# Two graph networks on one core: later key batches, sigmoids ahead of the sum copy, and another order of work at the networks' border

## What is computed

```python
h = relu(layernorm(x))
h = relu(h @ enc_w1.T + b) @ enc_w2.T + b            # encoder
for w in conv_w:                                     # 5 layers of one GRU cell
    agg = segment_sum((h @ w)[src], dst)
    r, z = sigmoid(...), sigmoid(...)                # from agg @ wih.T and h @ whh.T
    n = tanh(i_n + r * h_n)
    h = (1 - z) * n + z * h
x = x + sigmoid(relu(relu(h) @ dec_w1.T + b) @ dec_w2.T + b)   # decoder
g = relu(layernorm(x))                               # second network
g = relu(A @ g @ W1.T + b1)                          # A: adjacency with degree scales
x = x + A @ g @ W2.T + b2
```

## Time and profile before

| | us |
|---|---|
| runs (3) | 798.94, 802.02, 803.88 |
| median | 802.02 |
| the profiled execution's own time | 802.24 |
| its span in the trace | 799.7 |
| TensorE busy in the span | 735.3 |

### The profile page before, as it was taken

One profiled execution on the slowest core, in us unless ns is written; L12 is line 12 of the kernel. 1 busy time (PEld: TensorE's weight loads), 2 busy tenths in 40 slices (PEclk: granted clock), 3 DMA queues, 4 the chain that ended last, 5 costly groups with the idle time before them and its releaser, 6 DMA issues.

```text
span 799.7 us, 9315 instructions
## 1 busy us (share of the span) xinstructions
PE 735.3 (92%) x3802; PEld 375.1 (47%) x3802; DVE 329.2 (41%) x652; ACT 322.9 (40%) x446; POOL 39.2 (5%) x49
## 2 busy tenths in 40 slices
PE   2379999899989999999999999999997799999996
PEld 2256656434534445444444444444444445555443
DVE  4999998452402325032250322545645521213101
ACT  0378988662433425243262422523345411221000
POOL 4300000000000000000000000120011210000000
PEclk9989999999999999999999999999999999999999
DMA  6000010342310224003140031420002000000001
GB/s 170 7 1 2 1 70 2 55 100 46 70 23 1 60 54 75 11 7 73 35 83 2 14 66 35 85 80 1 1 0 97 1 1 1 1 1 2 26 14 44
DMA packets 78553, 28.37 MB, mean 35 GB/s; under 512 B 70100, under 2 KB 77653, under 8 KB 78378
## 3 DMA queue, kind: packets, MB, share of 16 engines
q1 hardware_dynamic: 75738, 26.01, 15.1%
q10 hardware_dynamic: 2528, 1.06, 0.6%
q0 software_dynamic: 240, 0.66, 0.3%
HBM read 8.03 MB, written 2.60 MB: 13 GB/s over the span
## 4 chain that ended last, share of the span: by engine, by line
PE 78%; DVE 11%; ACT 5%; DMA 3%; issue 2%; SPq 1%; POOL 0%; ACTq 0%; DVEq 0%
PE PSA L1134 30%; PE PSA L1287 15%; PE PSA L1213 5%; DVE CT L799 4%; PE PSA L1146 3%; PE PSA L1157 3%; PE PSA L1155 3%; PE PSA L1148 3%; PE PSA L1154 3%; PE PSA L1150 3%; PE PSA L1080 3%; DMA H<-yS 2%; PE PSA L1275 2%; PE PSA L1263 1%; ACT AT L1444 1%
## 5 line engine op out<-in xcount | busy, mean ns | idle before, releaser
L1134 PE MATMUL PSA<-AT,H 128*128 128x512 fp8e3 (+1 forms) x1522 | 287.5, 348 | 5.6 <-DMA H<-yS 4.8
L1134 PEld LDWEIGHTS PSA<-AT,H 128*128 128x128 f16 x1522 | 131.5, 98 | 163.8 <-issue 12.6
L1002 DVE SCALAR_TENSOR_TENSOR rS<-PSA,bias,rS 128x512 f32<-128x512 f32 (+1 forms) x35 | 23.9, 682 | 292.4 <-ACT rS L1528 292.4
L1487 ACT ACTIVATE aggS<-PSA 128x512 f32<-128x512 f32 (+1 forms) x35 | 19.1, 545 | 216.4 <-PE PSA L1157 206.2
L1444 ACT ACTIVATE AT<-PSA 128x1000 fp8e3<-128x1000 f32 (+1 forms) x79 | 92.2, 1235 | 26.1 <-PE PSA L1080 26.0
L799 DVE TENSOR_TENSOR CT<-CT 128x2048 bf16<-128x2048 bf16 x80 | 92.4, 1203 | 6.1 <-PE PSA L1080 4.7
L1418 ACT ACTIVATE CTL<-AT 128x3125 fp8e3<-128x3125 fp8e3 (+1 forms) x25 | 69.9, 2795 | 0.0
L1080 PE MATMUL PSA<-CT 128*128 128x125 bf16 x625 | 47.6, 230 | 21.1 <-DVE CT L799 18.0
L1287 PE MATMUL PSA<-CT,H 128*128 128x512 fp8e3 (+1 forms) x336 | 66.9, 357 | 0.0
L1287 PE MATMUL PSA<-CT,AT 128*128 128x512 fp8e3 (+1 forms) x336 | 66.7, 357 | 0.0
L1080 PEld LDWEIGHTS PSA<-CT 128*128 128x128 bf16 x625 | 41.6, 102 | 34.7 <-DVE CT L799 23.7
(11 more groups left out here) (162 smaller groups left out, 645.3 us busy)
## 6 DMA issues: line engine op xcount, KB each, us to landing
AT<-scale_scratch SPq DMA_DIRECT2D x1, 1562.5 KB, 6.3
H<-in_x SPq DMA_DIRECT2D x1, 1536.0 KB
out<-AT SPq DMA_DIRECT2D x6, 256.0 KB
comb_scratch<-CT SPq DMA_DIRECT2D x1, 960.0 KB, 4.1
comb<-comb_scratch SPq DMA_DIRECT2D x5, 192.0 KB, 2.8
H<-yS SPq DMA_TRANSPOSE x48, 2.5
H<-in_x SPq DMA_DIRECT2D x1, 512.0 KB, 6.8
CT<-AT SPq DMA_TRANSPOSE x25, 4.0
```

Source lines behind the costliest of these rows:

```text
L1134: last = nc.tensor.matmul(bank[:, 0:w], H16[:, l % 2, t, h, :], AT3[:, t, n0:n0 + w], start=(t == 0 and h == 0), stop=(t == T - 1 and (h = ...
```

## The change

Keys 1 to 4 are made in blocks 4, 10, 16 and 23 and not in 1 to 4; their transposes use the bank of the encoder's second product (EC2), so that TensorE waits for the encoder's or the combination's copies before them, and those wait for the key copies. One sigmoid of a single column is put ahead of the layers. In every iteration the sigmoids r and z of chunk c-1 come ahead of the sum copy `aggregated(c)`. At the end of the last layer the gates of chunk 5 come ahead of the decoder's first product of chunk 4; the decoder's products of chunks 4, 5 and 6 stand in other places between the partial sums; ScalarE casts the f16 high halves of chunks 0 to 2 (a new semaphore `input2_hi_early` tells GpSimd), VectorE those of 3 to 6; `last_pairs` of chunks 5 and 6 and `second_input` of chunk 4 move. In the second network ScalarE expands a chunk before it copies the projection of the one before; at the outputs two banks (TB, IB) and two tiles (`aggS`, `rS`) take turns, and the check's matmul comes earlier.

Left out below: renamed arguments of the key calls, the new semaphore's line, and waits that say the same as the text.

```diff
@@ -200,6 +200,9 @@
...
 SUM1, SUM2 = (1, 0, 6), (0, 7, 1)
+EARLY = 3
+turned_bank = lambda c: PS[(TB, IB)[c % 2]]
+summed2 = lambda c: (aggS, rS)[c % 2]
 OUT = late([P, TL, F], F32)
@@ -230,7 +233,8 @@
...
 ENC = 2
-KEYS_AT = range(1, KW)
+KEYS_AT = {4: 1, 10: 2, 16: 3, 23: 4}
+assert all(b + 1 < k * (PW // J) for b, k in KEYS_AT.items())
 PART = {16: (0, 4), 18: (0, 5), 20: (0, 6)}
@@ -834,7 +838,7 @@
...
         if b in KEYS_AT:
-            keys(b)
+            keys(KEYS_AT[b])
         if b == 1:
@@ -917,8 +921,6 @@
...
     def high_half(c):
-        if c == 0:
-            dve.wait_ge(sum_ready, L * NC)
         dve.wait_ge(input2_ready, CU[c][0] + CU[c][1])
@@ -970,7 +972,7 @@
...
                 last = nc.vector.scalar_tensor_tensor(
-                    OUT[0:k, t0 + j, :], PS[TB][0:k, j * F:j * F + F], dinvU[0:k, t0 + j:t0 + j + 1],
+                    OUT[0:k, t0 + j, :], turned_bank(c)[0:k, j * F:j * F + F], dinvU[0:k, t0 + j:t0 + j + 1],
                     X32[0:k, t0 + j, :], ALU.mult, ALU.add)
@@ -991,9 +993,6 @@
...
                     added_loops(g)
-            if l == L - 1 and c == NC - 1:
-                for c1 in range(4):
-                    high_half(c1)
             if 1 <= c <= NC:
@@ -1004,7 +1003,9 @@
...
                 nc.vector.tensor_tensor(rS[:, 0:w], PS[IB][:, 0:w], rS[:, 0:w], ALU.add).then_inc(new_input, 1)
-            if l == L - 1 and 2 <= c < NC:
+            if l == L - 1 and c == NC - 1:
+                high_half(EARLY)
+            if l == L - 1 and 2 <= c < NC - 1:
                 decoder_bias(c - 2)
@@ -1029,12 +1030,14 @@
...
                 checked_loops()
+            if l == L - 1 and c == NC - 1:
+                decoder_bias(c - 2)
             if l == L - 1 and 2 <= c < NC:
...
             if l == L - 1 and c == NC:
+                decoder_bias(c - 2)
                 high_half(4)
-                decoder_bias(c - 2)
                 decoded(c - 2)
@@ -1061,11 +1064,13 @@
...
             pe.wait_ge(ident_set, 2)
+        else:
+            pe.wait_ge(state_encoded, (1, 4, NC, NC)[k - 1])
+        if k == KW - 1:
+            pe.wait_ge(comb_copied, L)
         pe.wait_ge(keys_ready, k + 1)
-        if k >= 1:
-            pe.wait_ge(keys_copied, k)
         for h, v in enumerate((pf, kf)):
-            last = nc.tensor.transpose(PS[KEYB][0:SL, h * PW:(h + 1) * PW], v[:, k, :], ident[0:PW, 0:PW])
+            last = nc.tensor.transpose(PS[EC2][0:SL, h * PW:(h + 1) * PW], v[:, k, :], ident[0:PW, 0:PW])
         last.then_inc(keys_transposed, 1)
@@ -1106,6 +1112,7 @@
...
                 pe.wait_ge(state_encoded, s - 1)
+            pe.wait_ge(keys_copied, 1 + sum(k < off + ENC for k in KEYS_AT))
             nc.tensor.matmul(PS[EC2][:, 0:w1], enc2, rS[:, 0:w1], start=True, stop=True).then_inc(enc2_product, 1)
@@ -1201,13 +1208,13 @@
...
         if g == 0 and q == 0:
-            pe.wait_ge(keys_copied, KW)
+            pe.wait_ge(rows_found, 1)
         if g == 0 and q == 1:
...
         if g == 0 and q == 3:
-            pe.wait_ge(comb_copied, L)
+            pe.wait_ge(keys_copied, KW)
         for t in range(t0, t0 + nt):
@@ -1240,13 +1247,15 @@
...
                 aggregate(agg_bank(q), w, n0, l, ready=ready, between=between).then_inc(sum_ready, 1)
-            if l == L - 1 and 2 <= c:
+            if l == L - 1 and 2 <= c < NC - 1:
                 decode1(c - 2)
...
                 permute_scales()
-            if l == L - 1 and 2 <= c:
+            if l == L - 1 and c == NC - 1:
+                decode1(c - 2)
+            if l == L - 1 and 2 <= c < NC - 1:
                 decode2(c - 2)
@@ -1297,18 +1306,19 @@
...
     partial_sum(SUM1[0], 0, V16, 1, input2_lo)
+    decode2(NC - 3)
     gates(L - 1, L * NC - 1, NC - 1)
     partial_sum(SUM1[0], 0, V16, 2, input2_lo)
+    partial_sum(SUM1[0], 0, V16, 3, input2_lo)
     decode1(NC - 2)
-    partial_sum(SUM1[0], 0, V16, 3, input2_lo)
-    decode2(NC - 2)
     pe.wait_ge(sum_copied, L * NC)
     partial_sum(SUM1[1], 1, V16, 0)
+    partial_sum(SUM1[1], 1, V16, 1)
+    decode2(NC - 2)
+    partial_sum(SUM1[1], 1, V16, 2)
     decode1(NC - 1)
-    partial_sum(SUM1[1], 1, V16, 1)
+    partial_sum(SUM1[1], 1, V16, 3)
     decode2(NC - 1)
-    partial_sum(SUM1[1], 1, V16, 2)
-    partial_sum(SUM1[1], 1, V16, 3)
     for g in (4, 5):
@@ -1339,10 +1349,10 @@
...
         pe.wait_ge(sum2_copied, c + 1)
-        pe.wait_ge(output_ready, c) if c else pe.wait_ge(sum1_scaled, NC)
+        pe.wait_ge(output_ready, c - 1) if c >= 2 else pe.wait_ge((sum1_scaled, projected_lo)[c], NC)
         for u in range(u0, u0 + nu):
-            last = nc.tensor.transpose(PS[TB][0:rows2(u), (u - u0) * F:(u - u0 + 1) * F],
-                                       aggS[:, nodes(u, TC * P * c)], ident[:, :])
+            last = nc.tensor.transpose(turned_bank(c)[0:rows2(u), (u - u0) * F:(u - u0 + 1) * F],
+                                       summed2(c)[:, nodes(u, TC * P * c)], ident[:, :])
         last.then_inc(sum2_transposed, 1)
@@ -1363,6 +1373,9 @@
...
     partial_sum(SUM2[2], 2, Z16, 1)
+    pe.wait_ge(late_ones_set, 2)
+    pe.wait_ge(check_ready, 1)
+    nc.tensor.matmul(PS[RB][0:1, 0:4], onesL[:, 0:1], chk[:, 0:4], start=True, stop=True).then_inc(check_summed, 1)
     pe.wait_ge(projected_packed, 64)
@@ -1372,9 +1385,6 @@
...
     last_pairs_sum(SUM2[2], 2, ZP, sum2_ready)
-    pe.wait_ge(late_ones_set, 2)
-    pe.wait_ge(check_ready, 1)
-    nc.tensor.matmul(PS[RB][0:1, 0:4], onesL[:, 0:1], chk[:, 0:4], start=True, stop=True).then_inc(check_summed, 1)
     turned(1)
@@ -1504,6 +1514,8 @@
...
             aggregated(0)
+    act.wait_ge(mhalf_set, 1)
+    nc.scalar.activation(lnb[:, 0:1], mhalf[:, 0:1], ACT.Sigmoid)
     act.wait_ge(gate_biases, 1)
@@ -1512,14 +1524,10 @@
...
                     degree(q - 3)
-                if l == L - 1 and c >= 1:
+                if l == L - 1 and 1 <= c < NC - 1:
                     last_pairs(c - 1)
-                if l == L - 1 and c == NC - 1:
-                    last_pairs(c)
-                if l == L - 1 and c >= 2:
+                if l == L - 1 and 2 <= c < NC - 1:
                     decode_hidden(c - 2)
-                if q >= 1:
-                    aggregated(q)
             if 1 <= c <= NC:
@@ -1532,6 +1540,10 @@
...
                                      ).then_inc(update_gate, 1)
+            if 1 <= q and c < NC:
+                aggregated(q)
+            if l == L - 1 and c == NC - 1:
+                decode_hidden(c - 2)
             if c >= 2 and l < L - 1:
@@ -1549,9 +1561,19 @@
...
                 decode_sig(c - 2)
-                second_input(c - 2)
+                if c == NC - 2:
+                    act.wait_ge(sum_ready, L * NC)
+                    for c1 in range(EARLY):
+                        u0, nu = CU[c1]
+                        nc.scalar.activation(V16[0:P, u0:u0 + nu, 0, :], hidden2(P, u0, nu), ACT.Copy
+                                             ).then_inc(input2_hi_early, 1)
+                    last_pairs(NC - 2)
+                    last_pairs(NC - 1)
+                if c < NC - 1:
+                    second_input(c - 2)
             if l == L - 1 and c == NC:
                 decode_hidden(c - 2)
+                second_input(c - 3)
                 decode_sig(c - 2)
@@ -1566,9 +1588,9 @@
...
                                      bias=bias[:, B_L1 + k:B_L1 + k + 1]).then_inc(expand_relu, 1)
-        if c >= 1 and c <= NC:
-            t0, nt = CU[c - 1]
-            act.wait_ge(project_product, c)
+        if c >= 2:
+            t0, nt = CU[c - 2]
+            act.wait_ge(project_product, c - 1)
             act.wait_ge(late_ones_set, 1)
@@ -1578,9 +1600,11 @@
...
         act.wait_ge(sum2_ready, c + 1)
-        if c >= 1:
-            act.wait_ge(sum2_transposed, c)
-        nc.scalar.activation(aggS[:, 0:w], PS[SUM2[c % 3]][:, 0:w], ACT.Copy, scale=1.0 / S0
+        if c == 1:
+            act.wait_ge(project_product, NC)
+        if c >= 2:
+            act.wait_ge(sum2_transposed, c - 1)
+        nc.scalar.activation(summed2(c)[:, 0:w], PS[SUM2[c % 3]][:, 0:w], ACT.Copy, scale=1.0 / S0
                              ).then_inc(sum2_copied, 1)
...
     with act.If(act.value_load(flag[0:1, 0:1], min_val=0, max_val=1000) > 0):
```

13 lines of the change are left out of this document (7 added, 6 removed).

## The result

The changed kernel took **779.16 us** in the median (777.5 to 779.66, 4 runs) against 801.5 (798.94 to 803.88, 4 runs) for the kernel before on the same chip: ratio 0.9706, interval 0.9682 to 0.973. Run again later it gave 778.04 (5 runs) against 803.51 (9 runs), ratio 0.9689 (0.9669 to 0.971). The prediction was 781.5, range 775 to 791. They differ in two places that count: at the border into the last layer the first waits 0.4 us longer, and at the border to the second network TensorE's clock falls once in the first and not in the second.

What follows compares the result with a forecast made beforehand. TensorE was taken to bound the kernel, busy 735.3 of 799.7 us, so only its idle or half-clock time could be won. Terms 3.1 + 4.1 + 3.2 + 6.0 + 0.45 + 4.1 = 20.95 gave 781.5 us, range 775 to 791.

Steps and rivals of the forecast that it cites:

- Part 1: Window blocks: later key batches let VectorE, which sets the pace there, run earlier; 3.1 us, bounds 0.5 to 4.5.
- The cover at block 16: Window blocks: VectorE's lead just covers key batch 3's 1.85 us there; failing would cost up to 1 us.
- Part 2: First gates: early sigmoids and table load close TensorE's gaps before chunks 1 and 2; 4.1 us, bounds 2.8 to 4.1.
- Part 3: Layer borders: ScalarE's f16 copy of chunk 4 starts earlier, shrinking four idle times; 3.2 us, bounds 1 to 4.8.
- Part 4: Networks' border: an earlier sigmoid r of chunk 5 brings the packing forward; 6.0 us, bounds 2 to 11.
- the walk to r of chunk 5: Networks' border, ScalarE: old durations put r at 616.3 instead of 622.54, 6.2 us earlier, and packing at 644.
- The rule on casts: Networks' border: skill's rule favours VectorE for elementwise work; by it ScalarE's three casts cost 0.5 us of the 6.0.
- Part 5: Second network: earlier expansion of chunk 5, 0.45 us; outputs with two banks and tiles, no gap or clock fall, 4.1.
- (a): Networks' border chain and layers' DMAs swallow more than walked, window gain also smaller; 789 us, chance 0.2.
- (b): TensorE's waits all go, at window blocks, layer borders and networks' border; 774 us, chance 0.1.
- (c): Window stage: TensorE's clock stays at its lower level, costing 28 us over five block pairs; 809 us, chance 0.02.
- (d): Table load stays put or early copies wait for a later product; inside Part 2's and Part 4's bounds, no own chance.

Runs made afterwards that it cites:

- first execution: One of two profiled executions of the changed kernel, with a clock fall at the border to the second network; 776.5 us of span.
- u1: Changed kernel with key batches put back to the first four blocks; block 12 starts at 73.94, end 3.10 us later than the first execution.
- u3: Changed kernel without the one-column sigmoid ahead of the layers; sums 0.66 us later, 0.54 left at the end, nothing visible in the median.
- u2: Changed kernel with the sum copy ahead of the two sigmoids again in every layer, early table load kept; 10 us slower in the median.
- second execution: The other profiled execution of the unaltered changed kernel, without a clock fall at the border to the second network; 775.0 us of span.
- e5: Changed kernel with GpSimd's first low halves held until VectorE has made chunk 3's scales; span 1.6 us below the first execution.
- u5: Changed kernel with TensorE's old order of gates and decoder products at the networks' border; no measurable difference in time.
- e8: Changed kernel with TensorE's ready partial sums put ahead of the wait for node chunk 5's low half; span gain 4.9 us against first execution, 3.4 against second execution.
- e6: Changed kernel with the three early f16 casts back on VectorE, behind chunk 3's scales; span 1.8 us below the first execution.
- u4: Changed kernel with the old outputs: one bank, one tile, check's product before chunk 1's transposes; waits from first transposes to end worth 3.17 us.
- e7: Changed kernel with key batches 1 and 2 behind blocks 6 and 13 in place of 4 and 10; 783.74 us, 5.0 slower in the trace.
- e11: Changed kernel with VectorE's f16 copy of chunk 5 ahead of chunk 6's residual addition; 0.5 us gained against the second execution.

## Why the prediction was right, point by point

The time lies 2.3 us below the forecast. That it is so near is in part luck: the parts missed by up to 1.8 us and made up for one another. The signs agree in the main, with three exceptions. A lower clock behind the new gap, named as a sign of being wrong, came in the first execution. Of the two gaps at the networks' border the first was 3.3 and the second 0 or 0.45, and GpSimd and the DMAs ended them. The border of layer 0 kept its 0.7 by another wait than the one meant, and the last border 1.20 or 0.81.

**Part 1** (3.1 forecast, 3.91 measured, some 3.5 of it left at the end by u1). The count of batches ahead of block 12 was right. Two sizes were off. By block 5 VectorE had won 6.0 and not 5.55: in the kernel before, one normalization (at 37.17) took 1.81 us, in the changed one all take 1.11. GpSimd was clearing tiles at that moment; that this was the cause is not shown. And 0.3 was lost again between block 12 and the first gates (4.22 to 3.91), where I had 0.6 for the later transposes. The cover at block 16 held.

**Part 2** (4.1, 4.63). Both gaps closed, as worked out. What I left out: each restart costs too. Without its idle time, a chunk's gates lasted 5.42 us from start to start (160.58 to 167.32 less 1.32), and now 5.15 (153.73 to 158.88). The three steps around the gaps add up to 0.54 so, the difference; that it is a restart of TensorE's pipeline is my reading of it, which no run separates. The lower bound of 2.8 was wrong in its reasoning: with the load on the path only 0.66 would be lost at the sums (0.96 behind the first border), not 1.3, as r moves ahead by more than the load lasts (u3).

**Part 3** (3.2, 5.03). By layer 2.14, 0.95, 1.00 and 0.94. The mechanism was right for the first three borders (undoing the order alone gives 4.5 of the five back, u2). The terms were too small: each closed gap of 0.5 gave 0.95 or 1.00, as in part 2 more than its idle time; and at layer 0 1.1 of 1.84 were to go, but the whole 1.84 went, and the border gave 2.14. The DMAs of chunks 4 and 5 were no limit there any more, and the 0.77 that is left was there before as 0.80. At the last border 1.1 of 1.86 were to go and 0.66 went, 1.05 in the second execution; why this border repeats less well is not shown.

**Part 4** (6.0, 4.58). This is the part that was too high, and its step that failed in size is the walk to r of chunk 5. "It ends at about 614.6, just when the scales are ready: hidden, with no slack": in the old timeline's terms the relu of chunk 3 started at 602.85 + 13.57 = 616.42, 1.8 late. The work on ScalarE in between was hidden; the scales were late. I had walked the chain with the old durations, 0.16 for each of VectorE's small operations, although the early casts also start GpSimd's low halves early, straight into them: 2 x 1.0 us (shown by e5: held back, 0.16 again). So r of chunk 5 started 4.6 earlier than before and not 6.2, and the packing was at 646.2 in the old timeline's terms and not at 644. Little of that reached the result, and this is luck: I had 5.6 to 6.1 us from the packing to the pair's product, and in the second execution it took 4.3. There part 4 is 5.64 (19.61 at the packed pair, less 13.97 at the last layer's first gates), 0.4 short of the forecast; the other 1.1 that the first execution lacks is the fall of the clock behind the new gap, which the forecast had only in its bounds. Nor did each of the two old falls cost the 1.7 that I took for it: behind the one at 612.7 TensorE waited again for ScalarE (1.77 and 2.48), and u5 shows a fall at such a place that costs nothing. That what counts is r of chunk 5 was right (u5: TensorE's own order is worth nothing), and so was the idle time before chunk 5's sums in kind; 3.3 instead of 2.4, and none at the packed pair, or 0.45. That this idle time wasn't forced is what I missed: ready sums stood behind it (e8). What the new places of the decoder's products, of `last_pairs` and of `second_input` are worth on ScalarE and VectorE one by one is not shown: no run undid them.

The rule on casts: moving them to VectorE did win (e6, 1.8 us of span), yet not by speed per element, which neither engine's timeline shows to matter (the Trainium skill states its factor of three for bf16; these casts read f32, 0.42 us alone against 0.6). The casts on ScalarE let GpSimd start too soon, and holding GpSimd back won the same with the casts left there (e5, 1.6).

**Part 5** (0.45 and 4.1; 0.26 and 4.84). The expansion of chunk 5 came 0.98 earlier and 0.72 was given back. At the outputs the waits gave 3.17 where I had 2.4 (2.14 at the gap with its restart, and 1.03 at the end, not 0.55), and the remaining 1.7 is the fall of the clock, which I had tied to the gap of 1.85. u4 has the gap and no fall. The sum was nearly right for that execution and the reason wrong: the gap does not bring the fall by itself.

**The rivals.** (a) and (b) did not come; (c) did not: the first execution has one short half-speed stretch at 46.17, the second none, and block 12 comes at 69.69 and 69.70; e7, with batch 1 two blocks later, has two such stretches. (d) did not: the table load went where it was sent.

## What to carry to other kernels

Look at what an in-order engine has ready but queued behind a wait: one copy moved behind two sigmoids was worth 10 us, TensorE's new order at the networks' border nothing, since a chain elsewhere set the end. When a step is moved earlier, ask which engine it sets going and what that one then runs beside; walk the chain again with those durations, not the old ones. In front of a wait that can't be shortened, put work that is ready. And before a difference of half a microsecond is put down to an edit, look at whether two executions of one kernel agree to that at the same place.

## What the runs showed of the hardware

- The fall of TensorE's granted clock behind a gap differs between executions of one kernel. Behind 3.32 us: with a fall in one, without in the other. Behind 1.85 at the outputs: with in the kernel before, without in u4. Behind 4.14 and 2.48 (before), 2.48 (u2) and 2.09 (u5): with. Behind 1.84 in u2 and 1.60 in e11: none. A fall costs 1.7 us where TensorE sets the pace, and nothing where it waits again soon after (u5). The kernel before had three between 612 and 760 us, the changed one one or none, so at most 3.4 to 5.1 us of the difference of these profiles hang on that. The Trainium skill, "TensorE: Matmul & The Clock Gate", Part 1, calls the warm-up at a kernel's start variable from run to run; the two executions show the same of a fall in the middle.
- VectorE beside a GpSimd subtraction: 0.16 became 1.11 and 1.08 (128 x 4), 0.69 became 1.33 and 1.42 (128 x 512, two SBUF inputs), 0.48 became 1.44. The reset gate's step, which reads PSUM, took 0.75 beside a low half in e5 as well as alone.
- A closed gap gives more than its idle time: 0.27 us more from one chunk's gates to the next, 0.4 more at the borders of layers 1 and 2.
- A table load took 1.28 us, and ScalarE's next instruction followed it within 0.02.
